# Attention: the mask of the row maxima added by VectorE in place of 32 products of TensorE a step

## The reference

```
q, k, v = split(xn @ W_qkv);  q, k = layernorm(q) * q_scale, layernorm(k) * k_scale   # over all 128 features
scores  = (q / sqrt(8)) @ k.T per head                  # 1024 x 1024
scores  = where(key later than query, finfo.min, scores)
out     = softmax(scores) @ v @ W_out
```

## Time and profile before

| | us |
|---|---|
| median of 3 runs | 3990.48 (3989.49 to 3993.26) |
| the profiled execution | 3989.54 |
| its span, first to last instruction | 3987.8 |
| TensorE busy in the span | 3691.3 (93%) |
| VectorE busy | 3204.8 (80%) |
| ScalarE busy | 2905.2 (73%) |
| GpSimd busy | 3061.3 (77%) |
| mean granted TensorE clock | 0.973 |

### The profile page before, as it was taken

One profiled execution on the slowest core, in us unless ns is written; L12 is line 12 of the kernel. 1 busy time (PEld: TensorE's weight loads), 2 busy tenths in 40 slices (PEclk: granted clock), 3 DMA queues, 4 the chain that ended last, 5 costly groups with the idle time before them and its releaser, 6 DMA issues. The chain is left out here.

```text
span 3987.8 us, 172955 instructions
## 1 busy us (share of the span) xinstructions
PE 3691.3 (93%) x65553; PEld 2532.0 (63%) x65792; DVE 3204.8 (80%) x6126; ACT 2905.2 (73%) x5873; POOL 3061.3 (77%) x3927
## 2 busy tenths in 40 slices
PE   4788888589999999999999999999999999999997
PEld 2333434257777777777777777777777777777775
DVE  7676666278888888888888888888888888888885
ACT  5465656467777777777777777777777777777775
POOL 4111111289999999999999999999999999999994
PEclk7799899799999999999999999999999999999999
DMA  2422220122222322222322223222232222222222
GB/s 80 69 37 33 29 30 9 50 73 66 66 64 66 92 63 63 63 63 69 85 63 63 63 64 93 65 65 66 64 91 63 63 63 63 74 65 65 66 65 58
DMA packets 176123, 250.55 MB, mean 63 GB/s; under 512 B 46726, under 2 KB 65796, under 8 KB 175108
## 3 DMA queue, kind: packets, MB, share of 16 engines
q1 hardware_dynamic: 176004, 248.94, 25.5%
HBM read 39.08 MB, written 8.39 MB: 12 GB/s over the span
## 5 line engine op out<-in xcount | busy, mean ns | idle before, releaser
L1041 PE MATMUL w_ring<-w_wqkv,w_xs 128*128 (+1 forms) x2304 | 1157.1, 605 | 24.7 <-DMA w_scales<-in_L_ffn_k_scale 19.8
L1432 POOL TENSOR_TENSOR w_qr<-w_raw,w_tc 128x512 f32<-128x512 f32 x384 | 488.9, 1273 | 174.6 <-PE w_ring L1061 168.2
L1446 POOL TENSOR_TENSOR w_qr<-w_qr,w_qrot 128x512 f32<-128x512 f32 x384 | 572.1, 1490 | 0.0
L1041 PEld LDWEIGHTS w_ring<-w_wqkv,w_xs 128*128 128x128 f32 x2304 | 379.4, 191 | 190.8 <-issue 163.0
L637 DVE TENSOR_REDUCE a_row_max<-a_ring 128x1 f32<-128x640 f32 (+6 forms) x352 | 353.3, 1028 | 178.7 <-PE a_ring L467 172.6
L1439 POOL TENSOR_TENSOR w_qrot<-w_raw,w_tc 128x512 f32<-128x512 f32 x384 | 485.8, 1276 | 0.0
L607 POOL TENSOR_SCALAR_AFFINE_SELECT a_probs<-a_probs 128x512 f32<-128x512 f32 x128 | 81.2, 634 | 502.0 <-ACT a_probs L572 502.0
L572 ACT ACTIVATE a_probs<-a_wide 128x512 f32<-128x512 f32 (+1 forms) x608 | 323.4, 573 | 184.2 <-PE a_wide L488 112.2
L1117 PEld LDWEIGHTS w_ring<-w_pts,w_vw 64*64 64x64 f32 x24576 | 376.7, 135 | 92.9 <-issue 92.9
L1232 ACT ACTIVATE w_ksq<-w_ring 128x512 f32<-128x512 f32 x384 | 229.3, 597 | 271.4 <-PE w_ring L1041 271.4
L1117 PE MATMUL w_ring<-w_pts,w_vw 64*64 64x32 f32 x24576 | 398.3, 220 | 4.2 <-issue 2.4
(11 more groups left out here) (157 smaller groups left out, 8551.7 us busy)
## 6 DMA issues: line engine op xcount, KB each, us to landing
w_vw<-w_v SPq DMA_DIRECT2D x1152, 128.0 KB, 2.3
w_vw<-w_v SPq DMA_DIRECT2D x768, 64.0 KB, 2.0
a_q_stack<-q_parts SPq DMA_DIRECT2D x144, 64.0 KB
a_k_stack<-k_parts SPq DMA_DIRECT2D x144, 64.0 KB
w_wqkv<-in_L_ffn_Wqkv SPq DMA_DIRECT2D x6, 1536.0 KB, 6.0
q_parts<-ap_parts SPq DMA_DIRECT2D x8, 384.0 KB, 3.5
k_parts<-ap_parts SPq DMA_DIRECT2D x8, 384.0 KB, 3.5
w_wo<-in_L_ffn_Wo SPq DMA_DIRECT2D x12, 256.0 KB, 3.4
```

The lines of the kernel that those rows point to most:

```text
L1041: nc.tensor.matmul(bank(what, i, u)[:], xs[u][:], rhs, start=True, stop=True).then_inc(done, 1)
L1432: nc.gpsimd.tensor_tensor(by_head(qr[i][:]), by_head(raw[i][:]), wide(table(u, Q_COS)), ALU.mult).then_inc(q_straight[i], 1)
L1446: nc.gpsimd.tensor_tensor(qr[i][:], qr[i][:], qrot[i][:], ALU.add).then_inc(q_added[i], 1)
```

## The change

In the maxima of TensorE the product with the mask goes. In the maxima of VectorE, the block on the diagonal of every head of the unit gets the mask added in place in PSUM, by one instruction that reads `masks[:, 0, :]` (fp32) once per head; the reduce then waits for that addition through a new semaphore `hidden`, which is cleared ahead of each unit. `mask_qk` and its copy go.

```
-        mask_qk = sb("mask_qk", [P, P], BF16)
...
-                nc.scalar.copy(mask_qk[:], masks[:, 0, :])
...
-        v_ready, link, moved = sem("v_ready"), sem("link"), sem("moved")
+        v_ready, link, moved, hidden = sem("v_ready"), sem("link"), sem("moved"), sem("hidden")
...
-                        nc.tensor.matmul(bank[:, at + k0:at + k0 + n_cols], q_stack[hg][0:96, h0 + i, c * P:(c + 1) * P],
-                                         k_stack[hg][0:96, h0 + i, k0:k0 + n_cols], start=True, stop=True)
-                    mm = nc.tensor.matmul(bank[:, at + width - P:at + width], ident_bf[:], mask_qk[:], start=False, stop=True,
-                                          skip_group_check=True)
+                        mm = nc.tensor.matmul(bank[:, at + k0:at + k0 + n_cols], q_stack[hg][0:96, h0 + i, c * P:(c + 1) * P],
+                                              k_stack[hg][0:96, h0 + i, k0:k0 + n_cols], start=True, stop=True)
                 mm.then_inc(r_full, 1)
...
                 h0, heads, c = max_units[n]
+                dve.sem_clear(hidden)
                 wait(dve, r_full, ring_at(b, hg, n) + 1)
                 src = slot(b, hg, n)[:, 0:heads * stride_of(c)].rearrange("p (h k) -> p h k", h=heads)[:, :, 0:(c + 1) * P]
+
+                diagonal = src[:, :, c * P:(c + 1) * P]
+                nc.vector.tensor_tensor(diagonal, diagonal, masks[:, 0, :].unsqueeze(1).broadcast_to([P, heads, P]), ALU.add).then_inc(hidden, 1)
+                dve.wait_ge(hidden, 1)
                 nc.vector.tensor_reduce(row_max[:, h0:h0 + heads, c:c + 1], src, AX.X, ALU.max).then_inc(r_done, 1)
```

## The result

The changed kernel takes 4034.4 us (median of 3 runs, 4026.73 to 4036.66) against 3990.48. The ratio is 1.0106, 95% interval 1.0091 to 1.012: slower, by 44 us where 47.5 were forecast. The profiled execution took 4036.66 us, its span is 4034.9.

The account below looks back on a forecast made before the run. VectorE was taken to bound each step's head and TensorE its tail; 45 us for fifteen steps, plus 7.5 for the first, less 5 for half-clock steps, gave +47.5 on 3990.5, 4038 us; 4010 to 4070 held eight in ten.

Parts of the forecast that it names:

- Only the attention stage changes: Only the stage from 112 to 750 us, sixteen steps, is touched; the windowed layers after it carry over unchanged.
- Head and tail: Between splits, VectorE paces the head (to M9, slack 1.7 us); TensorE paces the tail (M12 to M21).
- VectorE's idle time takes the adds: Attention steps: VectorE's 10 idle us absorb the 8.65 us added, only removed products show, 3960 us; chance 5%.
- the tail makes up the loss: TensorE recovers the head's loss in the tail, step stays near 35.4 us, about 3996 us; chance 5%.
- M11 starts 17.2 us into the step, the step is 38.4 us: Clean step: TensorE's start of unit M11 moves from 14.20 us by 3.0; splits 38.4 us apart, before 35.37.
- Rival 3: TensorE's clock halves more often in the heads: 2.3 us for ten more steps, 4061 us; chance 12%.
- The 5 us set off for steps that were at half clock before: Some seven steps at half clock in the head already hide up to 2 us of additions each; 5 off.
- Prices of the additions: VectorE's in-place adds: 0.691 us over four heads, 0.425 over two, 0.293 over one.
- the gap behind each: VectorE's wait between an addition and its reduce, taken at 0.04 us, bounds -0.10 to 0.17.
- The first step: Step without scores, VectorE busy 22.0 of 24.0 us: between 6.6 and 8.65 us show, 7.5 taken.
- The tail: From M11 to the split: removed products give back 0.35 us, M21's own addition and link cost 0.33.
- The signs named ahead: Profile after: TensorE's wait for reduces up 30 us or more, tail waits about 1.0, no VectorE wait from split to M9.

Follow-up runs that it names:

- e3_tail: Changed kernel with VectorE adding the mask for M10 to M20 only, TensorE's products doing the rest: 3980.35 us, 0.9985 of the kernel before.
- e5: Changed kernel with every addition of M10 to M20 done twice: 4041.44 us, 1.0131 of the kernel before.
- e2: Changed kernel with VectorE adding the mask for M0 to M9 only, TensorE's products from M10 on: 4024.28 us, 1.0091 of the kernel before.
- e6: Changed kernel with every addition of M0 to M9 done twice: 4112.93 us, 1.0296 of the kernel before.
- e4_filled: Changed kernel plus products that nobody reads where TensorE waits between split and M9: 4021.91 us, 1.0094 of the kernel before.
- e1_both: Changed kernel with TensorE's 32 mask products a step put back, so the mask is added twice: 4043.96 us, 1.0142 of the kernel before.
- e11: Changed kernel with VectorE's additions for M10 to M20 only, only in steps with scores, products elsewhere, no fill: 4002.46 us, 1.004 of the kernel before.
- e10: Changed kernel with VectorE's additions for M10 to M20 only, in all steps, plus unread products in TensorE's head waits: 3974.2 us, 0.9961 of the kernel before.
- e9: Changed kernel with VectorE's additions for M10 to M20 only, in steps with scores, plus unread products in the head: 3990.07 us, 1.0001 of the kernel before.
- e12: Changed kernel with six more semaphore clears on VectorE ahead of each unit of the first step: 4038.23 us, 1.012 of the kernel before.

## Why the prediction was right

- *Only the attention stage changes.* Right: +45.5 of +47.1 us of span. By terms: 45 - 5 = 40 forecast for the fifteen steps, 41.3 measured; 7.5 for the first, 5.3 measured; nothing for the rest of the stage, -1.1 measured.
- *Head and tail.* Right: the loss lies ahead of M11 in all fifteen steps, and the runs show it from both sides: e3_tail's and e5's additions cost next to nothing, e2's and e6's cost nearly all (outside the turns e2_head's steps are as long as the changed kernel's). The rival that VectorE's idle time takes the adds fell with e6 and e2, the one that the tail makes up the loss with the tail's 21.2 us before and after.
- *M11 starts 17.2 us into the step, the step is 38.4 us.* At full clock (e4_filled) it is 17.24 and 38.46. That it agrees so closely is in part luck: VectorE's wait of 0.32 us ahead of M2 stayed, which the sum had at nothing (and part of which is the clear, also taken at nothing), while the first operation of the split now takes 0.24 us in place of 0.43. In the changed kernel itself it is 17.8 and 39.0 in the step shown, and 17.5 and 38.7 at best in batches 1 to 3.
- *The clock.* Rival 3 took its fall as unlikely (12%) because the head is bound by VectorE. It came in every step, so the mechanism that was called unlikely is there. The argument against it was half right: most of it is hidden, and what showed was 0.2 to 1.0 us a step (e4_filled) in place of 2.3. Its price was also too high in another way: only seven steps had a clock of 1.00 before, so not ten more could fall.
- *The 5 us set off for steps that were at half clock before.* Right in its sign: the eight steps with a clock under 1.00 before grew by 1.9 us each in the mean, the seven with 1.00 by 3.7. Against 3.0 for each, the first take 8.5 us off and the second put 4.8 on, together -3.7 where -5 was taken. The size of the term was taken and not worked out from rows, so that it came this near is luck.
- *Prices of the additions.* 0.69 to 0.70, 0.42 to 0.43 and 0.29 to 0.30 us, as taken; the gap behind each is 0.03 where 0.04 was taken. On the other side a reduce and the addition behind it overlap by 0.08 (378.28 + 0.69 to 378.89), as two reduces did before; so this saves time only where a reduce of before stood behind a wait and overlapped with nothing.
- *The first step.* 7.5 forecast, 5.3 measured: 8.65 less the 2.0 of idle time, which went altogether, less 1.2 of that overlap, which the sum's lower bound of 6.6 did not have.
- *The tail.* Forecast -0.35 + 0.33, measured +0.06. The first term is 0.29 by e1_both.
- *The signs named ahead.* TensorE's wait for the reduces rose by 84 us where 30 or more was asked, and the tail's waits fell to 0.9 to 1.0. That VectorE would not wait between split and M9 did not come: 0.32 and 0.47 us are left.
- *Not in the prediction:* the loop's turns. The two steps behind them grew by 2.9 and 1.8 us, no more than the others, so the sum was not hurt; but VectorE's wait there that no engine ended was new, e2_head, which is without it, is 9 us shorter in these two steps than the changed kernel, and in e11 it made a faster edit slower.

On the links, the Trainium skill (VectorE: DVE Perf Modes, "The DRAIN you can't avoid") reports for eight chained copies that a semaphore after each costs nothing extra. Here an operation behind a wait starts 0.03 us after the end of the row before, and one without a wait 0.08 us ahead of it (the earlier trace rows have it behind an addition too: 329.47 + 0.42 to 329.81). By that the wait costs 0.11 us a link, 1.1 us for the ten links of a head, and what was measured on copies does not hold for this form. It could not be left out, since the reduce reads what the addition writes; no run prices it alone. The Trainium skill's warning on the clock (TensorE: Matmul & The Clock Gate, "HAM oscillation"), that idle stretches between bursts of products bring the half clock back, agrees with this trace: TensorE waits 84 us more for the reduces, every step has a clock under 0.93, and products that nobody reads in those waits bring it back to 1.00 outside the loop's turns and the first step.

## What to carry to other kernels

An engine's idle time is worth something only in the stretch in which it lies: split a step where the pace passes from one engine to the other, and move work into the stretch whose waits it can fill. Here the same additions are free behind M11 and cost nearly their full length before it. Made there alone, with TensorE kept busy in the head, they give 3974.2 us, 0.4% under the kernel before; most of that comes from the clock and from the two steps behind a turn of the loop, and not from the products saved. Where an engine's work gets fewer instructions but more waiting, look at its clock afterwards, and where a program has loops, at the steps behind each turn.

## What the runs showed of the hardware

- Products that nobody reads keep the clock up: with 42 of them a step the granted clock went from about 0.91 to 1.00 in all steps outside the loop's turns but the first, and with 27 in e10 likewise, where e3_tail had 0.95 or 0.96 in six of these twelve. No wait of VectorE grew by it in the steps shown.
- Behind a turn of the loop VectorE can stand idle for 13.6 us with no engine to wait for (e9, e11), for 5 to 7 us in one stretch (the changed kernel, e1, e4, e5, e6, e12), or not at all, and two kernels with the same loop (e3_tail and e11) differ in this. The number of instruction packets of one queue (42 or 43 against 53 to 57) tells whether such a wait is there.
- In-place additions in PSUM of 128, 256 and 512 columns take 0.29, 0.42 and 0.69 us, about 0.16 us and 1.04 ns a column. The operation that waits for one starts 0.03 us after its end; one that does not wait starts 0.08 us ahead of it.
